# Adding the experts' weighted answers in DRAM with accumulating scatters

## The reference, cut to what matters

```
t = t + attn(_ln_t(t))                       # tokens t: [16384, 256]
x = _ln_t(t)                                 # normalised tokens
probs = softmax(x @ router_w.T)              # 8 experts
rw, re = top_k(probs, 2);  rw = rw / rw.sum(-1)
combine = zeros(N, 8).at[n, re].set(rw)
out = x
for e in range(8):
    y = gelu(x @ w1[e] + b1[e]) @ w2[e] + b2[e]
    out = out + combine[:, e] * y
t = t + out                                  # then turned back to [4, 256, 64, 64]
```

## Time and profile before

| | |
|---|---|
| median of three runs | 1523.21 us (1523.09 to 1526.4) |
| the profiled execution | 1526.19 us |
| its span, first to last instruction | 1524.4 us |
| PE / DVE / ACT / POOL busy | 86% / 70% / 65% / 46% |
| mean granted TensorE clock | 0.914 of 2.4 GHz |
| read from and written to HBM | 136.80 MB and 117.80 MB |

### The profile page before, as it was taken

One profiled execution on the slowest core, in us unless ns is written; L12 is line 12 of the kernel. 1 busy time (PEld: TensorE's weight loads), 2 busy tenths in 40 slices (PEclk: granted clock), 3 DMA queues, 4 the chain that ended last, 5 costly groups with the idle time before them and its releaser, 6 DMA issues. The chain is left out here.

```text
span 1524.4 us, 29139 instructions
## 1 busy us (share of the span) xinstructions
PE 1311.8 (86%) x8812; PEld 1151.4 (76%) x8812; DVE 1065.8 (70%) x3724; ACT 994.5 (65%) x2124; POOL 703.8 (46%) x774
## 2 busy tenths in 40 slices
PE   3899999999999999999995199999999999924343
PEld 3788888888888888888875189999999999923232
DVE  5488888888888777877865666555555666537665
ACT  1678788887888778887764177776666667612222
POOL 3115554555545554454443346666666666620000
PEclk9999999999999999999996599999999999965555
DMA  7534554645543222231221655555555555449998
GB/s 276 187 91 116 146 143 119 174 109 153 142 137 109 95 95 91 88 107 66 74 81 57 230 176 164 162 162 162 165 165 168 164 167 167 154 171 420 421 420 331
DMA packets 118072, 252.29 MB, mean 166 GB/s; under 512 B 40608, under 2 KB 54176, under 8 KB 113568
## 3 DMA queue, kind: packets, MB, share of 16 engines
q1 hardware_dynamic: 82976, 159.94, 32.7%
q0 software_dynamic: 26112, 71.60, 13.2%
q10 hardware_dynamic: 8832, 18.89, 3.3%
HBM read 136.80 MB, written 117.80 MB: 167 GB/s over the span
## 5 line engine op out<-in xcount | busy, mean ns | idle before, releaser
L1627 POOL DMA_INDIRECT answers<-yy,dest_i x288 | 303.7, 1055 | 189.1 <-DVE dest_i L1741 116.9
L1492 POOL DMA_INDIRECT sent<-tn,slot_s x256 | 275.7, 1077 | 222.2 <-DVE slot_s L1315 150.0
L1753 DVE TENSOR_TENSOR xl<-m_bank,xh 128x512 fp32r<-128x512 f32 x144 | 93.0, 687 | 180.3 <-ACT xh L1723 180.2
L1717 ACT ACTIVATE hid<-m_bank,b1s 128x512 f32<-128x512 f32 x144 | 99.0, 689 | 135.6 <-issue 87.8
L1676 PE MATMUL s_bank<-band,hh 128*128 x576 | 166.9, 290 | 0.9 <-DVE yy L1770 0.9
L1850 PE MATMUL m_bank<-ident,tot 128*128 128x128 f32 x256 | 62.2, 424 | 117.3 <-ACT fin L1864 85.5
L1676 PE MATMUL s_bank<-band,hl 128*128 x576 | 160.7, 279 | 0.0
L1676 PE MATMUL s_bank<-w_s,hh 128*128 x576 | 160.6, 279 | 0.0
L1850 PEld LDWEIGHTS m_bank<-ident,tot 128*128 128x128 f32 x256 | 50.2, 223 | 129.1 <-issue 70.3
L738 PE MATMUL m_bank<-wvo,band 128*128 128x258 f32 x792 | 133.2, 304 | 13.2 <-DVE band L1300 10.8
L770 PE MATMUL o_bank<-vv,at 128*128 128x256 f32 x512 | 140.0, 396 | 1.3 <-DVE tt L1211 0.7
(11 more groups left out here) (211 smaller groups left out, 3549.1 us busy)
## 6 DMA issues: line engine op xcount, KB each, us to landing
xin<-sent SPq DMA_DIRECT2D x72, 516.0 KB, 3.8
got<-answers SPq DMA_DIRECT2D x32, 1024.0 KB, 8.2
xs<-in_x SPq DMA_DIRECT2D x32, 512.0 KB, 5.6
raw<-in_x SPq DMA_DIRECT2D x32, 512.0 KB
residual<-tt SPq DMA_DIRECT2D x32, 512.0 KB, 2.9
res<-residual SPq DMA_DIRECT2D x32, 512.0 KB, 9.8
out_x<-fin ACTq DMA_DIRECT2D x32, 512.0 KB, 8.7
answers<-yy,dest_i POOLq DMA_INDIRECT x288, 3.3
```

Source lines behind the costliest of these rows:

```text
L1492: eng.indirect_dma_start(sent, bass.IndirectOffsetOnAxis(slot_s[:, par, j, k:k + 1], 0), tn[:, par, k, :], None).then_inc(scattered[par], 16)
L1627: eng.indirect_dma_start(answers, bass.IndirectOffsetOnAxis(dest_i[:, slot, k:k + 1], 0), yy[:, slot, k, :], None).then_inc(rows_out[slot] ...
L1717: eng.activation(hid[:, f, :], h_bank[f][:, :], ACT.Gelu, bias=b1s[:, par, f:f + 1])\
L1753: eng.tensor_tensor(xl[:, par, c, :], xT_bank[c][:, :], xh[:, par, c, :].bitcast(f32), ALU.subtract).then_inc(xl_ready[c].sem, 1)
```

## The change

- The DRAM tensors residual and answers are replaced by one, sums, with a row per token and 1024 spare rows. Stage D stores the block's rows there, in the place of residual.
- The two weights of a token are computed in the first loop: VectorE takes the difference of the two best logits (fall), ScalarE its exponential (fell), and POOL in row_tails, ahead of a block's scatters, 1/(1+fell) and (fell-1)/(1+fell). With the token's number and best expert they go along in sent, whose rows grow from 258 to 260 numbers. The work on best and mix after the first loop is gone.
- NJ is 71 in place of 72.
- In the second loop the tile's weights are picked (pick) in stage X. VectorE multiplies the first two of yy's four parts in stage Y, ScalarE the other two in a new stage Z, one pass later. POOL scatters in stage Z, with an add: each row of yy is added to the token's row in sums. Within one expert no token occurs twice. Ahead of tile n POOL waits until the scatters of tile n-2 have landed, and those of n-1 if the two tiles are of different experts; the count it waits for is read from a table, turn_i.
- In the third loop SP loads 0.5 MB of sums per block (six slots), TensorE transposes it, VectorE copies one half and ScalarE the other, and ScalarE stores (four slots). There is no arithmetic left in it.

```diff
-    NJ = 2 * NT // BT + E
-    NJ += NJ % 2
+    NJ = 2 * NT // BT + E - 1
...
+                def fallen(it):
+                    route.wait(eng, it, "Dfall")
+                    tailed_rows.wait(eng, it.before(), "Em")
+                    eng.activation(fell[:, it.parity("D"), :], fall[:, :], ACT.Exp).then_inc(share.sem, 1)
...
+                def row_tails(it):
+                    pe, blk = it.parity("E"), it.block("E")
+                    share.wait(eng, it.before(), "De")
+                    if blk >= 2:
+                        eng.wait_ge(scattered[pe], it.pair("E") * (32 * KT))
+                    eng.tensor_copy(tn[:, pe, :, C], places[:, blk * KT:blk * KT + KT])
+                    eng.tensor_scalar(less[:, :], fell[:, pe, :], 1.0, -1.0, ALU.mult, ALU.add)
+                    eng.tensor_scalar(more[:, :], fell[:, pe, :], 1.0, 1.0, ALU.mult, ALU.add).then_inc(tailed_rows.sem, 1)
+                    tailed_rows.wait(eng, it, "Em")
+                    eng.tensor_tensor(tn[:, pe, :, C + 2], more[:, :], wholes[:, 0, 0:KT], ALU.pow).then_inc(tailed_rows.sem, 1)
+                    tailed_rows.wait(eng, it, "Ep")
+                    eng.tensor_tensor(tn[:, pe, :, C + 3], less[:, :], tn[:, pe, :, C + 2], ALU.mult).then_inc(tailed_rows.sem, 1)
...
+                eng.iota(so_far[:, :], pattern=[[16 * KT, TURNS], [0, YB]], base=16 * KT, channel_multiplier=0,
+                         allow_small_or_imprecise_dtypes=True).then_inc(jiota, 1)
...
+                follow(eng.tensor_tensor(same[:, :], expert_f[:, 1:NJ], expert_f[:, 0:NJ - 1], ALU.is_equal))
+                eng.scalar_tensor_tensor(turn_i[:, :], same[:, :], -16.0 * KT, so_far[:, 0:NJ - 1], ALU.mult, ALU.add)
...
-                    if it.runs("Y"):
-
-                        slot = it.block("Y") % YB
-                        alone(eng, (dest_int.sem, dest_int.count(it, "Yd")),
-                              *((y.sem, y.count(it, f"Yt{i}")) for i, y in enumerate(y_taken)))
+                    if it.runs("Z"):
+                        at_ = it.block("Z")
+                        slot = at_ % YB
+                        if at_ > 0:
+                            if at_ <= YB:
+                                eng.wait_ge(rows_out[(at_ - 1) % YB], 16 * KT)
+                            else:
+                                turn = eng.value_load(turn_i[0:1, at_ - 1:at_], min_val=16 * KT, max_val=16 * KT * TURNS)
+                                eng.wait_ge(rows_out[(at_ - 1) % YB], turn)
+                        if at_ > 1:
+                            eng.wait_ge(rows_out[(at_ - 2) % YB], ((at_ - 2) // YB + 1) * 16 * KT)
+                        alone(eng, (scaled_d.sem, scaled_d.count(it.before(), "Ys")), (scaled_a.sem, scaled_a.count(it, "Zs")))
                         for k in range(KT):
                             eng.indirect_dma_start(
-                                answers, bass.IndirectOffsetOnAxis(dest_i[:, slot, k:k + 1], 0),
-                                yy[:, slot, k, :], None).then_inc(rows_out[slot], 16)
+                                sums, bass.IndirectOffsetOnAxis(dest_i[:, at_ % RING, k:k + 1], 0),
+                                yy[:, slot, k, :], None, compute_op=ALU.add).then_inc(rows_out[slot], 16)
...
+                    if it.runs("Z"):
+                        slot, at_ = it.block("Z") % YB, it.block("Z") % RING
+                        y_taken[1].wait(eng, it.before(), "Yt1")
+                        for k in range(2, KT):
+                            last = eng.activation(yy[:, slot, k, :], yy[:, slot, k, :], ACT.Copy, scale=pick[:, at_, k:k + 1])
+                        last.then_inc(scaled_a.sem, 1)
...
+                        y_taken[0].wait(eng, it, "Yt0")
+                        for k in range(2):
+                            last = eng.tensor_scalar(yy[:, slot, k, :], yy[:, slot, k, :],
+                                                     pick[:, it.block("Y") % RING, k:k + 1], None, ALU.mult)
+                        last.then_inc(scaled_d.sem, 1)
...
+        GOT, FIN = 6, 4
+                        eng.dma_start(got[:, blk % GOT, :, :].rearrange(flat), sums_of(blk)).then_inc(got_in[blk % GOT], 16)
...
+                                last = eng.transpose(turned_bank(it, c)[:, k * P:(k + 1) * P],
+                                                     got[:, blk % GOT, k, c * P:(c + 1) * P], ident[:, :])
...
+                        eng.tensor_copy(fin[:, blk % FIN, 1, :], turned_bank(it, 1)[:, :]).then_inc(f_taken[1].sem, 1)
...
+                        eng.activation(fin[:, blk % FIN, 0, :], turned_bank(it, 0)[:, :], ACT.Copy).then_inc(f_taken[0].sem, 1)
```

More of the change, by code:

```diff
@@ L530, in hybrid @@
         wden = lb("wden", [P, KT])
-        tn = lb("tn", [P, 2, KT, C + 2])
+        tn = lb("tn", [P, 2, KT, CR])
         tnT = lb("tnT", [P, CC, BT])
         logit = lb("logit", [P, KT, E])
-        best = lb("best", [P, NB * KT, 8])
+        best = lb("best", [P, KT, 8])
+        fall = lb("fall", [P, KT])
+        fell = lb("fell", [P, 2, KT])
+        less = lb("less", [P, KT])
+        more = lb("more", [P, KT])
         besti = lb("besti", [P, KT, 8], u32)
@@ L653, in lower_parts, with blank_rows @@
                               ALU.subtract).then_inc(split, 1)
[L655 removed]
+        def blank_rows(eng, rows, other, landed):
             to = rows.rearrange("(p k) c -> p k c", k=KT)
             eng.dma_start(to[:, :, 0:C], blank[:, :, :].broadcast_to([P, KT, C])).then_inc(landed, 16)
[L659 removed]
+            eng.dma_start(to[:, :, C:CR], tail_id[:, other, :, :]).then_inc(landed, 16)
         def fill_tail(eng, e):
@@ L1538, in hybrid @@
         b2_in = sem("b2_in")
-        late = ExitStack()
-        RES = 3
-        res = late.enter_context(nc.sbuf_tensor("res", [P, RES, KT, C], f32))
-        res_in = [sem(f"res_in{i}") for i in range(RES)]
         loop2 = ExitStack()
@@ L1825, in body @@
-                        eng.wait_ge(got_in[slot], it.block("K") // RES * 16 + 16)
-                        for k in range(KT):
-                            last = eng.scalar_tensor_tensor(part[:, k, :], got[:, slot, k, 0, :],
-                                                            share[:, k, 0:1], res[:, slot, k, :],
-                                                            ALU.mult, ALU.add)
-                        last.then_inc(part_ready.sem, 1)
-                        part_ready.wait(eng, it, "Kp")
@@ L1832, in body @@
-                        for i in range(CC):
-                            f_full[i].wait(eng, it.before(), f"Kf{i}")
-                        for k in range(KT):
-                            last = eng.scalar_tensor_tensor(tot[:, par, k, :], got[:, slot, k, 1, :],
-                                                            share[:, k, 1:2], part[:, k, :],
-                                                            ALU.mult, ALU.add)
-                        last.then_inc(tot_ready.sem, 1)
-                tiles_loop(eng, NB, body)
@@ L1841, in _ @@
-            @block.tensor
-            def _(eng):
-                def body(it):
-                    if it.runs("K"):
-                        par = it.parity("K")
-                        tot_ready.wait(eng, it, "Kt")
-                        for c in range(CC):
-                            f_taken[c].wait_before(eng, it, f"Kk{c}")
-                            for k in range(KT):
-                                last = eng.transpose(m_bank[c][:, k * P:(k + 1) * P],
-                                                     tot[:, par, k, c * P:(c + 1) * P], ident[:, :])
-                            last.then_inc(f_full[c].sem, 1)
+                        blk = it.block("K")
```

194 lines of the change are left out of this document (87 added, 107 removed).

## The result

The changed kernel takes 1572.09 us (median of four runs, 1569.14 to 1575.51) beside 1524.81 us for the kernel before (1523.09 to 1526.89): a ratio of 1.031, 95% interval 1.028 to 1.034. It is slower; 1436 us and a range up to 1540 had been forecast.

A forecast was written before the change was run, and what follows sets the result against it. TensorE was taken to bound the expert loop and transfers the final loop. Span 1524.4 - 79.4 (last loop) - 6.5 (one tile) - 1.5 (borders) = 1437.0 us, so 1436 us measured; range 1424 to 1540.

The forecast's parts named there:

- The scatter itself: the open price: Expert loop, POOL: an adding scatter costs between the plain issue of 1.055 us and twice that; the plain price was taken.
- room of 1.215 us: Expert loop: POOL's issue may rise from 1.055 to 1.215 us before four scatters exceed the 6.46 us tile.
- break-even of 1.52 us: Expert loop: at an issue of 1.52 us the loss is 87 us, all of the gain.
- The second rival: POOL's issue follows three accesses a row in place of two: 1.58 us, tile 7.93 us, 1540 us; chance 0.13.
- the 0.4 us for register load and waits: Expert loop: POOL's added register load and two or three waits cost about 0.4 us a tile.
- Last loop 88 us: Final loop: without residual loads and with the others halved, 82.2 us of transfers plus 6 us head and tail, saving 79.4 us.
- Borders -1.5: End of routing stage: VectorE's weight chain goes, so the expert loop starts 1.5 us earlier (bounds 0 and 3.6).
- Scalings hidden: Expert loop: two multiplications each on ScalarE and VectorE per tile cost nothing; uncovered, up to 1 us a tile, 71 us.
- One tile -6.5: Expert loop: 71 tiles in place of 72 save one tile of 6.46 us, taken as 6.5 us.
- Scatter issue, counted at nothing: Expert loop: adding scatters issue at the plain 1.055 us, so POOL adds nothing to the tile.
- Landing, taken at 3.5 us: Expert loop: scatters land 3.5 us after issue; at 7 expert changes POOL starts 1.2 us late, absorbed in two tiles.
- The third: Rival: adds don't pipeline in the DMA engines, full from 3.2 times 0.35 us; at five times 1610 us; chance 0.10.

The follow-up runs named there:

- adds of half rows: Changed kernel with adds of 128 rows of 512 bytes in place of 1024, into a table of their own; ratio 0.998 to the kernel before, on another chip.
- 64-row kernels: Changed kernel scattering 64 rows in place of 128: with adds, ratio 0.971 on another chip; as plain writes, 1436.86 us beside 1525.88 for the kernel before.
- plain version: Changed kernel with its four scatters per tile as plain writes in place of adds; 1439.46 us, ratio 0.944 to the kernel before.

## Why the prediction was wrong

**The step that failed** is "The scatter itself: the open price". Its bounds were right (1.055 us to twice that, measured 1.608), as were its room of 1.215 us and its break-even of 1.52 us. The value taken inside them was the lower end, with the reason that it is the nearest row, and that the routing's scatters, with longer rows, cost the same. Those rows have 258 numbers beside 256, so they could show nothing even of bytes; only the adds of half rows showed that bytes cost POOL nothing. Neither row says anything of a price per operation, and that was the question. The second rival (an issue of 1.58 us, a tile of 7.93, 1540 us) had the issue's size, with a chance of 0.13; its tile is 7.65, since the 0.4 us for register load and waits don't show, and it lacked the 43 us of waits. Its reason, a price that follows the number of accesses of each row, fell for the most part with the 64-row kernels, so its closeness is partly luck.

**The sum, term by term** (span 1437.0 forecast, 1571.2 measured):

- Last loop 88 us: 86.3. Right, and so are the halved loads at full engines.
- Borders -1.5: the second loop starts 2.0 us earlier, but in the two executions of the changed kernel it starts at 865.5 and 862.8 us, and with 71 tiles and the old border at 862.9. So no run shows this gain.
- Scalings hidden: right by the plain version, whose tile is 6.46 to 6.52 us with both in it. Single scatters of 1.2 us or more were to be more frequent if VectorE's multiplications lock POOL out, by "SBUF — State Buffer" (Who interferes with whom) of the Trainium skill; in the plain version 64 scatters overlap a multiplication, and none of them takes over 0.97 us. The runs speak against such a cost here; whether the multiplications ran in the two-port mode that the rule is about, no row shows. The 1.43 us that the prediction put beside this rule is the subtraction hl: 59 scatters of 288 took over 1.2 us before and 4 of 284 in the plain version, where only 17 start during hl. That is also why the plain mean fell from 1.055 to 0.972 us.
- One tile -6.5, and the loop at 482.9: the plain version took 488.8. The starts span 4.1 us less than before, so a part of the tile's gain is there, but the first scatter comes 26.6 us after the loop's start in place of 22.7 (26 to 27 in every kernel with stage Z, 22.7 to 24.2 in those without); these 3.9 us of filling were not counted.
- Scatter issue, counted at nothing: 86 us, of which about 14 by the lengthened scatters.
- Landing, taken at 3.5 us with the delay at changes "absorbed in two tiles": the pause from the last scatter's start to the next tile's is 6.2 to 6.7 us with adds and 4.3 to 5.6 without (4.5 from 1046.13 to 1050.65 in the plain version), and nothing absorbs it once POOL has no slack: 7 x 4.6 = 32 us. This followed from the failed step; a delay is absorbed only by the engine that isn't the bound.
- The first tiles, where each waits for the one before whatever the experts: 11 us. The rule stood in the code and was not priced.

**The rivals.** The third (adds that don't pipeline, 1610 us) came near in the transfers' time, 3.06 times 0.35 us, just below the 3.2 at which the engines fill and well below the five times behind its 1610 us, but the half-row adds kept the tile with a third less engine time: the transfers are no bound. The chance of 0.23 for slower was too low for an operation of which no row existed, at a break-even of 1.44 times the plain price with bounds of 1 and 2.

## What to carry to other kernels

Before moving work into an operation that the profile has no row of, work out the break-even price; where it lies between the bounds, the forecast is open, and the nearest row decides only if it varies the thing in question. For an engine that issues transfers, count issue time plus the gap against the tile; here its time followed its instructions and not their bytes. Use the median for the price of one and look beside which other engine's work the longer ones start. Where a chain of waits ends at buffers that a busy engine frees, look whether that engine ever stands idle before asking for more buffers; and a wait is only free while the engine that makes it has slack.

## What the runs showed of the hardware

- An indirect scatter that adds holds POOL for 1.56 us (128 rows) or 1.40 us (64), a plain one for 0.96 or 0.90; half as many bytes change nothing. The rise is for the most part a price per instruction. Why stays open.
- A scatter that starts while VectorE subtracts two SBUF tiles of 128x512 is longer, by up to 0.5 us (64 of 72 before, 41 of 51 in the changed kernel); elsewhere 3 of 449 in these two are longer by over 0.1 us.
- The add triples packets (143 against 48) and DMA engine time (1.07 against 0.35 us) at the same counted bytes; with half the bytes it is 0.69 us with as many packets. The counts are close to one packet per row and 16 more for an add (143 and 80), and one per four rows and 16 more for a plain scatter (48 and 32).
- TensorE's granted clock in the last loop was 0.72 in the changed kernel and 0.50 before, with the same 256 transposes in half the time: TensorE does nothing but transposes there, and the clock still rose to its upper level for part of it, after it had fallen to the lower one while TensorE stood idle:

```profile
1470.00:1480.00 10.00, 0.00 (x0) 0.00 (x0) 0.00 (x0) 0.00 (x0) 7.08 (x5) 0.50 0.66 74
...
1495.00:1500.00 5.00, 1.90 (x16) 1.42 (x14) 0.66 (x2) 0.56 (x2) 0.00 (x0) 1.00 1.03 413
1500.00:1510.00 10.00, 5.01 (x24) 3.99 (x24) 1.61 (x3) 1.33 (x3) 0.00 (x0) 0.56 1.04 414
```
